# Two-layer gated cross-attention: the second layer's attention on f16 halves that DMA transposes, three rounds in flight

## The reference, cut to what matters

```python
x = x + tanh(g_xattn[0]) * L0_xattn(layernorm(x), ctx, ctx, mask, ...)   # 8 heads, 256 "tokens" of 8
x = x + tanh(g_ffn[0])   * L0_ffn(layernorm(x), router, gate, up, down)  # 8 experts, top-p weights
x = x + tanh(g_xattn[1]) * L1_xattn(layernorm(x), ctx, mask2)            # third step
x = x + tanh(g_ffn[1])   * L1_ffn(layernorm(x), gate_up, down)           # fourth: token i goes to expert i % 4

def L1_xattn(h, mem, mask):                       # per sequence: 64 x 256, 64 x 256, 64
    scores = einsum('bsd,bmd->bsm', h, mem) * 256 ** -0.5
    scores = where(mask[:, None, :], scores, -1e30)
    readout = einsum('bsm,bmd->bsd', softmax(scores), mem)
    return where(any(mask), readout, 0)
```

## Time and profile before

| | |
|---|---|
| time, median of 3 runs | 859.29 us (858.58 to 860.84) |
| the profiled execution's own time | 859.4 us |
| its span in the trace | 857.6 us |
| PE, DVE, ACT, POOL busy | 90%, 80%, 69%, 68% |
| granted TensorE clock, mean | 0.958 |

### The profile page before, as it was taken

One profiled execution on the slowest core, in us unless ns is written; L12 is line 12 of the kernel. 1 busy time (PEld: TensorE's weight loads), 2 busy tenths in 40 slices (PEclk: granted clock), 3 DMA queues, 4 the chain that ended last, 5 costly groups with the idle time before them and its releaser, 6 DMA issues. The chain is left out here.

```text
span 857.6 us, 30114 instructions
## 1 busy us (share of the span) xinstructions
PE 772.9 (90%) x11511; PEld 719.4 (84%) x11511; DVE 687.2 (80%) x2385; ACT 595.8 (69%) x1298; POOL 580.2 (68%) x617
## 2 busy tenths in 40 slices
PE   3455689999999999999999999999999999888886
PEld 2343479999999998999999999999999999777875
DVE  3576778888888888888888888888888886898973
ACT  3267768877787877787887878787878773454442
POOL 4255637788879797979797888888888674222321
PEclk9657689999999999999999999999999999999999
DMA  7579999879998989898898889897888864120002
GB/s 234 166 146 235 237 230 206 149 140 158 150 162 143 156 150 148 157 142 161 147 172 138 167 138 165 137 176 143 152 153 154 128 107 135 51 63 14 26 4 97
DMA packets 319540, 122.99 MB, mean 143 GB/s; under 512 B 274716, under 2 KB 312612, under 8 KB 319396
## 3 DMA queue, kind: packets, MB, share of 16 engines
q1 hardware_dynamic: 318656, 120.53, 73.5%
q10 hardware_dynamic: 740, 0.54, 0.2%
HBM read 45.53 MB, written 8.39 MB: 63 GB/s over the span
## 5 line engine op out<-in xcount | busy, mean ns | idle before, releaser
L591 POOL TENSOR_TENSOR p_parts<-p,p_parts 128x512 f16<-128x512 f32 x256 | 296.7, 1159 | 114.3 <-ACT p_parts L706 103.2
L846 PE MATMUL psG<-xT,w_gu 128*128 128x128 f16 x3072 | 193.5, 220 | 7.2 <-DVE th_ga_h L1282 6.8
L583 POOL TENSOR_TENSOR hp_lo<-th_ga_h,hp_hi 128x512 f16<-128x512 f32 x136 | 157.7, 1160 | 57.2 <-ACT hp_hi L728 54.0
L846 PE MATMUL psU<-xT,w_gu 128*128 128x128 f16 x3072 | 192.2, 219 | 1.4 <-DVE th_ga_h L1290 1.3
L846 PEld LDWEIGHTS psG<-xT,w_gu 128*128 128x128 f16 x3072 | 176.3, 98 | 11.9 <-DVE th_ga_h L1282 9.7
L846 PE MATMUL psY<-w_dn,hp_hi 128*128 128x256 f16 x1024 | 181.7, 273 | 0.8 <-POOL hp_lo L583 0.8
L846 PEld LDWEIGHTS psU<-xT,w_gu 128*128 128x128 f16 x3072 | 175.4, 98 | 3.2 <-DVE th_ga_h L1290 2.6
L706 ACT ACTIVATE p_parts<-p 128x512 f16<-128x512 f32 x256 | 160.6, 627 | 6.1 <-DMA p_turn<-p_parts 5.6
L1206 DVE CUSTOM_DVE_ANT_0 ps<-ps,mask_in 128x256 f32<-128x256 f32 x256 | 104.2, 448 | 55.2 <-PE ps L846 54.6
L698 ACT ACTIVATE p<-ps,exp_bias 128x256 f32<-128x256 f32 x256 | 106.9, 469 | 48.1 <-DVE exp_bias L1210 46.8
L846 PE MATMUL psY<-w_dn,hp_lo 128*128 128x256 f16 x512 | 139.6, 273 | 0.0
(11 more groups left out here) (180 smaller groups left out, 1089.5 us busy)
## 6 DMA issues: line engine op xcount, KB each, us to landing
mask_in<-in_mask_Bx2048x_ff SPq DMA_DIRECT2D x32, 256.0 KB, 3.0
part_scratch<-parts SPq DMA_DIRECT2D x16, 384.0 KB, 4.0
q_stack<-part_scratch SPq DMA_DIRECT2D x62, 96.0 KB
k_stack<-part_scratch SPq DMA_DIRECT2D x62, 96.0 KB
stage<-in_L_ffn_gate_w SPq DMA_DIRECT2D x8, 512.0 KB, 4.4
stage<-in_L_ffn_up_w SPq DMA_DIRECT2D x8, 512.0 KB, 4.4
stage<-in_L_ffn_down_w SPq DMA_DIRECT2D x8, 512.0 KB, 4.4
p_turn<-p_parts SPq DMA_TRANSPOSE x256, 3.7
```

The source lines that it names most:

```text
L583: pool.tensor_tensor(hp_lo[:, u % 2, :], hb32[:, u % 2, :], hp_hi[:, u % 2, :], ALU.subtract).then_inc(s["h_split"], 1)
L591: pool.tensor_tensor(p_parts[:, g % 4, 1, :, :], p32[:, g % 2, :, :], p_parts[:, g % 4, 0, :, :], ALU.subtract).then_inc(s["plo_done"], 1)
L846: return pe.matmul(out_, lhsT, rhs, start=start, stop=stop, skip_group_check=shares_bank)
```

## The change

The second layer's round is written anew; the first layer and the units stay as they are.

- x (after the norm), the context and the probabilities are cut into f16 high and low parts (ACT writes the high part, POOL subtracts for the low part), and one DMA issued by SP transposes both parts. The f32 transposes on PE and ACT's copies out of PSUM go. Scores are 12 f16 products instead of 4 f32 ones with 128 columns, the readout is 6 instead of 2 with 256 columns.
- Both norms of a round are done by ACT with a scale and a bias. For that DVE writes the negated mean (`cnm`), and POOL multiplies it with the inverse deviation (`csh`). `x4T` is read by the second FFN with a step of four elements.
- A round starts four groups earlier (`late_base`) and has its last step at r = 10 instead of 7. Its steps stand at: stats r = -2, context high r = -2 and low r = -1, norm r = -1, low part and the two transposes r = 0, scores r = 3, Exp r = 4, transposing the probabilities r = 5, readout r = 7, `late_attend` and second statistics r = 8, second norm r = 9, its low part and its transpose r = 10. So `late_attend` of a round stays in the group in which it was.
- SP issues, in the group where a round's x and context are turned, those two before the probabilities of the round ahead, whose turn comes one group later.
- `Y_OUT_AT` and `Y_TURN_AT` move, the weight cut on ACT comes one group earlier.

```diff
-Y_OUT_AT = [8 * TAIL_STEP + at for at in (26, 33, 37, 44)]
-Y_TURN_AT = [8 * TAIL_STEP + at for at in (32, 36, 38, 45)]
+Y_OUT_AT = [8 * TAIL_STEP + at for at in (26, 30, 36, 44)]
+Y_TURN_AT = [8 * TAIL_STEP + at for at in (27, 31, 37, 45)]
...
-            return 8 * TAIL_STEP + 4 * t
+            return 8 * TAIL_STEP - 4 + 4 * t
...
+            def turn_pc(t):
+                sp.wait_ge(s["pl_lo"], t + 1)
+                if t:
+                    sp.wait_ge(s["read_done"], t)
+                turn_late(pT[:, :, :, :].rearrange("p a u t -> p (a u) t"),
+                          pc_parts[:, :, :, :].rearrange("p a u t -> p (a u t)"), "pl_turned")
...
+                        if r == 0:
+                            turn_ctx(t)
+                            turn_xn3(t)
+                            if t + 2 < ROUNDS:
+                                load_late_ctx(t + 2)
+                        elif r == 5:
+                            turn_pc(t)
+                        elif r == 10:
+                            turn_xn4(t)
...
+            def late_low(t, kind):
+
+                pool.wait_ge(s[f"xn{3 + kind}_hi"], t + 1)
+                parts_of, full = (xn3_parts, xn4_parts)[kind], (xn3, xn4)[kind]
+                pool.tensor_tensor(parts_of[:, 1, :, :], full[:, :, :], parts_of[:, 0, :, :], ALU.subtract
+                                   ).then_inc(s[f"xn{3 + kind}_lo"], 1)
...
+            def late_norm(t, kind):
+                act.wait_ge(s[f"pow{3 + kind}_done"], t + 1)
...
+                for u in range(2):
+                    act.activation(full[:, u, :], x_res[:, 2 * t + u, :], ACT.Identity,
+                                   scale=crs[:, kind, u:u + 1], bias=csh[:, kind, u:u + 1]
+                                   ).then_inc(s[f"xn{3 + kind}_ready"], 1)
+                act.wait_ge(s[f"xn{3 + kind}_ready"], 2 * t + 2)
+                act.activation((xn3_parts, xn4_parts)[kind][:, 0, :, :], full[:, :, :], ACT.Copy
+                               ).then_inc(s[f"xn{3 + kind}_hi"], 1)
...
-                            last = mm(bank[:, e * P:e * P + P], d_gu[:, wp, e, kt, i0:i0 + P], x4T[:, k, xp, kt, e, :],
+                            last = mm(bank[:, e * P:e * P + P].rearrange("p (t u q) -> p t u q", t=2, u=2),
+                                      d_gu[:, wp, e, kt, i0:i0 + P],
+                                      x4T[:, k % 2, :, xp, :, kt, :].rearrange("p t u (q e) -> p e t u q", e=NE1)[:, e],
...
-                dve.tensor_scalar(cve[:, kind, :], cmv[:, kind, :, 1], EPS, None, ALU.add).then_inc(s[f"ln{3 + kind}_in"], 1)
-
-            def late_norm(t, kind):
-                dve.wait_ge(s[f"pow{3 + kind}_done"], t + 1)
...
-                    dve.tensor_scalar((xn3, xn4)[kind][:, u, :], x_res[:, 2 * t + u, :], cmv[:, kind, u, 0:1],
-                                      crs[:, kind, u:u + 1], ALU.subtract, ALU.mult).then_inc(s[f"xn{3 + kind}_ready"], 1)
+                st.link(dve.tensor_scalar(cnm[:, kind, :], cmv[:, kind, :, 0], -1.0, None, ALU.mult))
+                dve.tensor_scalar(cve[:, kind, :], cmv[:, kind, :, 1], EPS, X_SCALE ** -2, ALU.add, ALU.mult
+                                  ).then_inc(s[f"ln{3 + kind}_in"], 1)
...
+                dve.tensor_scalar(low_bias[:, t % 2, :], low[:, t % 2, :], LOG_P_SCALE, None, ALU.add
+                                  ).then_inc(s["sc_masked"], 1)
```

More of the change, by code:

```diff
@@ L70 @@
 X_SCALE = 256.0
+C_SCALE = 16.0
 G_UNSCALE = 1.0 / (W_SCALE * X_SCALE)
@@ L221, in build @@
         cve = lb("cve", [P, 2, 2], F32)
+        cnm = lb("cnm", [P, 2, 2], F32)
         crs = lb("crs", [P, 2, 2], F32)
-        low = lb("low", [P, 2], F32)
-        csum = lb("csum", [P, 2], F32)
+        csh = lb("csh", [P, 2, 2], F32)
+        low = lb("low", [P, 2, 2], F32)
+        low_bias = lb("low_bias", [P, 2, 2], F32)
+        csum = lb("csum", [P, 2, 2], F32)
         valid = lb("valid", [P, 2], F32)
@@ L760, in late_exps @@
             def late_exps(t):
                 act.wait_ge(s["sc_masked"], t + 1)
+                if t:
+                    act.wait_ge(s["pl_lo"], t)
+                    act.wait_ge(s["pl_turned"], 16 * t)
                 for u in range(2):
-                    act.activation(pc[:, u, :], psV[:, u * P:u * P + P], ACT.Exp, bias=low[:, u:u + 1], scale=-1.0,
-                                   accum_out=csum[:, u:u + 1]).then_inc(s["c_exp"], 1)
-            def late_x_high(t):
-                act.wait_ge(s["xn4T"], t + 1)
-                for u in range(2):
-                    at = t % 2 * 64 + 32 * u
-                    act.activation(x4T[:, t // 2, 0, :, :, at:at + 32],
-                                   psM[:, u * D:u * D + D].rearrange("p (k q e) -> p k e q", k=KT, e=NE1),
-                                   ACT.Copy, scale=X_SCALE).then_inc(s["xn4_hi"], 1)
+                    act.activation(pc[:, u, :], ps1[:, 0, u * P:u * P + P], ACT.Exp, bias=low_bias[:, t % 2, u:u + 1],
+                                   scale=-1.0, accum_out=csum[:, t % 2, u:u + 1]).then_inc(s["c_exp"], 1)
@@ L997, in _ @@
             last.then_inc(s["router_T"], 1)
-            def late_turn(bank, src, done):
-                for u in range(2):
-                    for k in range(KT):
-                        at = (u * KT + k) * P
-                        last = pe.transpose(bank[:, at:at + P], src[:, u, k * P:k * P + P], ident[:, :])
-                last.then_inc(s[done], 1)
             def late_unit_in(u, bank, which, done):
@@ new lines, in late_scores @@
+            def late_scores(t):
+                pe.wait_ge(s["xn3_turned"], 16 * (t + 1))
+                pe.wait_ge(s["cx_turned"], 16 * (t + 1))
+                if t == 0:
+                    pe.wait_ge(s["exp_done"], 2 * 8 * B)
+                else:
+                    pe.wait_ge(s["c_exp"], 2 * t)
+                for u in range(2):
+                    j = 0
+                    for k in range(KT):
+                        for xp, cp in ((0, 0), (1, 0), (0, 1)):
+                            last = mm(ps1[:, 0, u * P:u * P + P], x3T[:, xp, u, k, :], cxT[:, cp, u, k, :],
+                                      start=(j == 0), stop=(j == 5))
+                            j += 1
+                last.then_inc(s["sc_done"], 1)
@@ new lines, in late_read @@
+            def late_read(t):
+                pe.wait_ge(s["pl_turned"], 16 * (t + 1))
+                if t == 0:
+                    pe.wait_ge(s["pv_evac"], B)
+                else:
+                    pe.wait_ge(s["x3_done"], 2 * t)
+                for u in range(2):
+                    for j, (pp, cp) in enumerate(((0, 0), (1, 0), (0, 1))):
+                        last = mm(psV[:, u * D:u * D + D], pT[:, pp, u, :], cx_parts[:, t % 3, cp, u, :],
+                                  start=(j == 0), stop=(j == 2))
+                last.then_inc(s["read_done"], 1)
```

231 lines of the change are left out of this document (114 added, 117 removed).

## The result

The kernel after takes 881.58 us (median of 4 runs, 880.45 to 884.39) against 859.21 beside it: a ratio of 1.0261, 95% interval 1.0240 to 1.0282. Slower was forecast, and 863.6; the range ended at 872.

The account below looks back on a forecast made before the run. DVE's queue was taken to set the late rounds' pace, with PE close behind. Stretch A +2.05, B +2.3 and C nothing gave +4.35 on the profiled 859.4, forecast 863.6 us, range 849 to 872.

Parts of the forecast that it names:

- PE at nothing: Late rounds: PE loses f32 transposes and products and gets 18 f16 products per round; counted as 0, DVE being behind.
- stretch A: From the gate of unit 116 to the end of the last first-FFN addition (803.60 us before): forecast +2.05 us.
- C: From the gate of unit 134 to the span's end, 18.2 us before: nothing counted.
- B: The last round, from the last first-FFN addition to the gate of unit 134, 35.8 us before: forecast +2.3.
- rival 3: Before unit 134's gate, TensorE's clock falls in PE's waits, slowing four matmul groups: +6.0, 869.6 us; chance 0.14.
- when the last x_res comes: Last round: late_attend of round 7 ends its x_res at T + 29.0, where before it was T + 29.4.
- The 9.1 from x_res to the gate: Last round: statistics, power and product, Identity and cut, low part, transpose and hops put unit 134's gate at T + 38.1.
- The weight cuts: Rounds 0 to 3: DVE's weight cuts wait for POOL's low parts, 1.35 per round, +5.4 us; bounds per round 0 and 2.3.
- The small instructions: Late rounds on DVE: seven small instructions held by POOL, 0.31 each, 2.15 us per round; bounds 0 and 9.3.
- The wait for the scores: Late rounds on DVE: this wait goes, 0.66 us per round, as scores use transposes ordered three groups earlier.
- The DVE model: DVE's queue sets the late rounds' pace; per round 3.78 us go, 0.8 and 2.15 come, net -0.83, five rounds -4.15.

Follow-up runs that it names:

- e1: Kernel after, with the second FFN's gate and up products reading x4T with a step of one: 869.44 us, ratio 1.0113 to the kernel before.
- e2: Kernel before, with the second FFN's gate and up products reading x4T with a step of four elements: 878.17 us, ratio 1.0207.
- e5: e1 with the first two copy-outs of the second FFN's sums in front of the second norms of rounds 5 and 6 on ScalarE: 866.63 us, ratio 1.0082.
- e10: e5 and e8 together on e1, copy-outs in front of the norms and PE kept busy in the last two waits: 865.11 us, ratio 1.0062.
- e14: e10 plus 12 or 14 unread 256-column products in front of eight groups of units 122 to 130: 863.41 us, ratio 1.0040.
- e8: e1 plus unread 512-column products, 18 before the down product of unit 133 and 14 before the gate of 134: 866.59 us, ratio 1.0073.
- e9: e1 with the second layer's norms back on VectorE, the cuts that follow them staying on ScalarE: 880.07 us, ratio 1.0232.
- e12: Kernel before with the second layer's norms on ScalarE and ScalarE's weight cuts one group earlier: 861.41 us, ratio 1.0020.
- e6: Kernel before with only the second layer's norms moved to ScalarE, at the same groups: 867.18 us, ratio 1.0077.
- e3: Kernel before, with the second FFN's gate and up products reading x4T with a step of two elements: 861.28 us, single run.
- e4: Kernel before, with the second FFN's gate and up products reading x4T with a step of eight elements: 938.06 us, single run.

## Why the prediction was wrong

The direction came out, the time didn't. By its steps (T is the end of the last first-FFN addition):

- **PE at nothing, in stretch A and C.** This is the step that failed. "As DVE is behind, I count nothing" took x4T's products at their old price, and so did "nothing counted" for C. Sixteen groups cost 23.1 us of PE more (23.6 + 23.6 busy against 12.1 + 12.0), 1.44 each, of which 12.7 came through to the end: four stand in C (22.99; in e1, without the step but partly at half clock, 19.14), eight in B and four at the end of A, where PE now runs without a pause from 793.90 to 824.86. The step of four was seen, but as an aside to rival 3 and for the four groups of C alone, with the remark that no row shows one. Priced for all sixteen it would have been the largest term of the sum. The rule that the prediction took from the Trainium skill's "SBUF — State Buffer", section "Door 1" (two accesses per 16 bytes for the full rate), doesn't hold for these products: with a step of four, which is two accesses per 16 bytes, e2 shows half the rate (23.6 us against 12.1).
- **Stretch B, when the last x_res comes.** Forecast T + 29.0, in the kernel after T + 38.1, in e1 (no step) T + 31.7. Of the 2.7 left over, the queue that I had not laid out was ScalarE's first copy-out behind the norm of round 5, and the half clock behind PE's wait for it (0.54 from 824 to 828 in e1): the prediction names only the second copy-out, in B, and the second-to-last, in C. With no step and the first two copy-outs in front of the norms, the last x_res comes at T + 29.2, 30.0 and 29.3 (e5, e10, e14) and the gate of unit 134 at T + 38.2, 39.0 and 38.2, where 29.0 and 38.1 were forecast; the last Exp, forecast to end at T + 19.6, begins at T + 19.1 in e5. So the layout of B comes out once the step and this queue are gone. The 9.1 from x_res to the gate came out at 9.0.
- **Rival 3, the clock.** It is real: 0.50 from 850 to 858 in the kernel after. But in the kernel after it costs these groups nothing, since a step of four takes 2.95 at 1.00 and 2.94 at 0.50. It costs once the step is gone (C is 1.8 shorter in e8 than in e1), and it falls in the late rounds too, where I had not looked for it.
- **Stretch A, POOL holding DVE.** The weight cuts: forecast +5.4, measured 12.22 - 7.6 = +4.6. The small instructions: forecast 2.15 per round, measured 0.7 (their calls above the shortest sum to 2.3 for `cnm`, 1.05 for the mask, 1.7 for `low_bias` and 0.5 for `cr` in eight rounds): mis-sized, most calls stay at their shortest. The wait for the scores, which the sum let go, is 8.9 instead of 4.4, as shown above. For five rounds these two errors are about -7 and +8, so they nearly cancel. Without the step, A is 93.14 to 94.66 in e1, e5, e8 and e10, 2.3 to 3.9 above before, beside 2.05 forecast; at the gate of unit 127, before any product with a step, these four and the kernel after stand 1.8 to 3.8 late. That the forecast comes near is luck: of its terms only the weight cuts were right, and part of the delay is clock (0.79 from 758 to 766).
- **The DVE model.** That norms on VectorE would cost some 2 us per round in this order is shown by e9 (+1.2%, 10.2 us in stretch A). That taking them away pays is not: e12 is no faster than before.
- **Two readings that carry no term.** The 1.26 us of SP's transposes is their median, not their bound (1.23 to 3.71). And the 12 f32 products that PE loses per round are records of the trace; by the code they are 6.

By ratios, the 2.6% (22.4 us) of loss are: step 12.7, copy-out and clock of the last round 4.4, clock in the late rounds about 1.9 (not clear of noise), and 3.4 that e14 still has. By e14's trace that rest lies in A (+1.3) and in B (+2.5, where the prediction's layout gave +2.3), less 1.0 in C; no run takes its causes apart. Whether the held weight cuts lie in it stays open.

## To carry to other kernels

A transposing DMA that saves engine work fixes the order of the columns; look at what step the consumer then reads with, and price every product that reads so, not only those on the last chain. In an engine's queue, an instruction that waits for a slow chain belongs behind whatever others need and is ready: weight cuts behind a norm cost 0.6% here (e6 against e12), a copy-out behind one some 0.3%, at the edge of what the runs can tell. Where PE waits in front of a chain of products, read the granted clock behind the wait before trusting their durations.

## What the runs showed of the hardware

The f16 moving operand's step (the operand that streams through TensorE, here x4T): a step of 4 bytes is nearly free (e3, 12.4 us against 12.1), and 8 and 16 bytes take 1.95 and 3.7 times as long as 2 (e2 and e4, 23.6 and 45.0 us). At a step of 8 bytes a group takes 2.95 us at a granted clock of 1.00 and 2.94 at 0.50 (kernel after), so at 2.4 and at 1.2 GHz alike. At a step of 16 bytes the granted clock was 0.59 from 800 to 840 us in e4, with PE busy all the time.
